# A four-layer graph network: where the own-node terms of two SAGE layers are made, and which engine adds two bias rows

## The chip, the cores and the metric

The kernel runs on one core of one Trainium2 chip. The metric is the device time of the whole program in microseconds, the median of three runs. Three executions took 5216.58, 5223.72 and 5224.33 us.

TensorE multiplies matrices out of SBUF into PSUM, which has eight banks of 512 fp32 columns by 128 partitions. VectorE, ScalarE and GpSimd do the rest; GpSimd issues the indirect DMAs that gather rows. All data here are fp32.

## The reference, cut to what matters

There are 3125 nodes with 128 features and 50000 edges sorted by destination. Four networks follow each other, each with a residual and a layer norm: a message MLP, two graph attention layers, three SAGE layers, and a softmax aggregation with a small MLP. The third and the fourth matter here:

```python
def sage_conv(h, Ws, Wn, b):
    agg = segment_sum(h[edge_src], edge_dst, num_segments=n)
    return h @ Ws + (agg * inv_deg) @ Wn + b
h = relu(sage_conv(x, Ws0, Wn0, b0))     # 128 -> 256
h = relu(sage_conv(h, Ws1, Wn1, b1))     # 256 -> 256
h = relu(sage_conv(h, Ws2, Wn2, b2))     # 256 -> 128
x = layernorm(x + h)
...
h = relu(agg @ mlp_w.T + mlp_b)          # agg: the softmax-weighted sum over a node's edges
x = layernorm(x + (h * scale + x))
```

The own-node terms are `h @ Ws`; they need no neighbour.

## The kernel before, in words

Nodes lie in 26 tiles of 128; features are kept by rows (`x_sb`, `y_sb`, `h_sb`: node on the partition) or turned (`xT` and the six planes of `big`: feature on the partition). Edges lie in 391 blocks of 128. A merge path of 416 steps, 104 groups of four, pairs each block with the node tiles that its edges end in.

**A SAGE pass** (`sum_pass`). GpSimd gathers the source rows of one block with one indirect DMA (L476) from a table in HBM into a ring of 13 groups of four in `big`. Before it refills a ring place it waits on the semaphore `summed`:

```python
if j >= n:
    pool.wait_ge(freed, at + j - n + lag)
```

With n = 13 and a lag of 8, gather group j needs the group six before it to be summed. ScalarE makes, for each step, a 128x128 matrix that marks which edge ends in which node (L882: squared distances, four a group; L888: one minus that, clipped at zero), in two buffers, so it waits for `summed` of the group two back. TensorE multiplies it with the gathered rows (L785) and lets the sums stay in banks 0 to 6 (`node_sums`) over the whole pass. In sage1 the rows have 256 columns; the second half goes through bank 7 (L790), and VectorE adds it to `y_sb` (L1166). In sage0 and sage2 bank 7 and VectorE have nothing to do.

**Between the passes** TensorE fills one of the banks 0 to 3 in turn (`fill`, a ring of four, `RING`), and the engine that the list `STAGES` names for the stage reads it. `fill` waits until the reader of four fills back is done.

- After sage0: VectorE scales the sums (L1537), TensorE turns them (`aT`, L542), ScalarE copies them into `big[0]` (L871). Then `sh0`: 16 fills of 128x416, each of two matmuls, `Ws0` with `xT` and `Wn0` with the turned sums (L533); ScalarE adds the bias `sb0` and clips (L1029) into `big[4]` and `big[5]`. Then `p1`, the products with `Wn1` (L519), copied by ScalarE (L866) and written to HBM as the table of sage1.
- After sage2: VectorE scales the sums of all packs of four tiles (L1537); then `out2`: per tile two products with `Ws2` (L519) and the bias row as a product of a row of ones with `b_sb` (L522); VectorE adds the scaled sums (`join_sage`, L1564) and the residual (`add_residual`, L1569). The layer norm (`norm`) follows: row sum (L1259), centring (L1265), squares on ScalarE (L948), their sum (L1270), square root on ScalarE (L950), scaling into `x_sb` (L1279). `in_packs` runs these steps over seven packs (six of four tiles, one of two) in a staggered order. `x_sb` is then written as the table of the next pass.
- At the end (`last`), per pack: VectorE bounds and inverts the totals (L1579, L1583), divides (L1587); TensorE turns (L830), ScalarE copies (L1049), TensorE multiplies with `mlpT` (L836) and adds the bias row as a product (L837) for each of four tiles; ScalarE clips into `y_sb` (L1050); VectorE scales (`scale_output`, L1593), adds the residuals (`add_both_residuals`, L1597), and the norm follows; the result is written out.

The order on each engine is the order of the code; semaphores tie the engines together. `weights_loaded` counts three loads at the start (16 each): the weights, the two bias rows `b_sb` (1 KB), and `r_sb`, rows spread over all partitions.

## Time and profile before

| | |
|---|---|
| median of three runs | 5223.72 us |
| the profiled execution | 5251.98 us, span 5250.2 us |
| TensorE matmul busy | 3245.7 us (62%) |
| VectorE busy | 2924.6 us (56%) |
| ScalarE busy | 2771.9 us (53%) |
| GpSimd busy | 2886.8 us (55%) |
| pass of sage0 | from 2458.7 to 3042.6 us |
| pass of sage2 | from 3796.0 to 4374.9 us |
| last stretch | from 5172.0 us |

The profile is of one execution. Times in its rows are microseconds from the span's start. A group's idle time is that of its engine just before it, and the name behind the arrow is what ended it; "remote" is a releaser that the profile does not name, "issue" is time in which the engine waited for nothing that it shows. A matmul of fp32 data appears as two records, so x32 are 16 matmuls. PEclk is the granted clock of TensorE as a share of 2.4 GHz; it is 0.5 or 1.0 at any time, and a window's figure is a mean.

### The profile page before, as it was taken

What the parts mean: (1) busy time and instruction counts of PE and PEld (TensorE: products, weight loads), DVE (VectorE), ACT (ScalarE), POOL (GpSimd) and SP (SyncE); (2) the same over time, 40 slices, a digit from 0 to 9 for tenths busy, and PEclk for the clock granted to TensorE, in tenths of its full rate; (3) what the DMA queues carried; (4) which work ended last, traced back from release to release, by engine and by line L of the source; (5) the groups of instructions that cost most, each with busy time, mean ns of one, the idle gap of its engine ahead of it and who ended that gap; (6) DMA issues with size and microseconds to landing.
All of it is one profiled execution on the core that took longest, in us unless ns stands there. A gap on an engine that the chain in (4) does not pass through costs nothing.

```text
span 5250.2 us, 70737 instructions
## 1 busy us (share of the span) xinstructions
PE 3245.7 (62%) x16464; PEld 2658.9 (51%) x16465; DVE 2924.6 (56%) x6078; ACT 2771.9 (53%) x5854; POOL 2886.8 (55%) x2818
## 2 busy tenths in 40 slices
PE   4666667778885778884233364555723335777776
PEld 3555554667774667673223244444522324655554
DVE  3666674999997999996000001112100003999997
ACT  1656664777774777773333333333323332777773
POOL 3455521666663666663666625666166662666661
PEclk7888888665555665555555577777855555999996
DMA  4344421223332323321111122333111111333331
GB/s 141 110 118 120 121 75 35 76 76 78 78 78 52 76 76 77 76 75 42 43 46 47 45 64 76 91 91 89 30 44 46 47 45 39 97 98 96 96 98 30
DMA packets 326787, 385.94 MB, mean 74 GB/s; under 512 B 68200, under 2 KB 267806, under 8 KB 326270
## 3 DMA queue, kind: packets, MB, share of 16 engines
q0 software_dynamic: 102496, 236.78, 16.2%
q1 hardware_dynamic: 221910, 142.28, 9.8%
q10 hardware_dynamic: 2218, 4.94, 0.3%
q8 instruction: 73, 1.20, 0.1%
q14 instruction: 90, 0.74, 0.0%
HBM read 366.52 MB, written 17.21 MB: 73 GB/s over the span
## 4 chain that ended last, share of the span: by engine, by line
PE 31%; another core or an unknown queue 21%; DVE 17%; issue 15%; ACT 11%; DVEq 3%; DMA 1%; SPq 1%; ACTq 0%; POOL 0%
PE ps L737 6%; ACT onehot L882 5%; DVE big L1166 4%; PE ps L595 4%; PE ps L686 3%; PE ps L724 3%; ACT onehot L888 2%; DVE w_run L1344 2%; DVE y_sb L1166 2%; PE ps L716 2%; PE ps L790 2%; PE ps L785 2%; PE ps L519 2%; DVE big L1369 2%
## 5 line engine op out<-in xcount | busy, mean ns | idle before, releaser
L476 POOL DMA_INDIRECT big<-table_sage,src_block x1173 | 1110.3, 947 | 852.5 <-issue 331.6
L462 POOL DMA_INDIRECT rows<-table_gat,src_idx x832 | 924.4, 1111 | 746.3 <-PE ps L659 278.5
L882 ACT ACTIVATE onehot<-iota,dst_rel 128x128 f32<-128x128 f32 x1664 | 530.6, 390 | 1400.5 <-remote 1031.4
L785 PE MATMUL ps<-big,onehot 128*128 x2496 | 536.1, 385 | 789.9 <-ACT onehot L888 459.9
L785 PEld LDWEIGHTS ps<-big,onehot 128*128 128x128 f32 x2496 | 476.2, 283 | 847.2 <-issue 842.5
L737 PE MATMUL ps<-y_sb,onehot 128*128 128x136 f32 (+2 forms) x2496 | 664.2, 425 | 81.5 <-DVE big L1166 73.5
L1537 DVE TENSOR_TENSOR y_sb<-ps,inv_row 128x512 f32<-128x512 f32 (+1 forms) x14 | 8.0, 645 | 1226.3 <-PE ps L785 1226.3
L462 POOL DMA_INDIRECT rows<-table_pool,src_idx x416 | 480.5, 1155 | 311.6 <-PE ps L663 119.6
L1166 DVE TENSOR_TENSOR big<-big,ps 128x257 f32 (+3 forms) x1664 | 576.2, 346 | 87.1 <-PE ps L737 24.9
L737 PEld LDWEIGHTS ps<-y_sb,onehot 128*128 128x128 f32 x2496 | 516.3, 278 | 143.9 <-DVE big L1166 118.0
L476 POOL DMA_INDIRECT big<-table_mlp,src_block x391 | 370.8, 948 | 344.0 <-DVE ps L1186 186.4
L888 ACT ACTIVATE onehot<-onehot,ones 128x512 f32<-128x512 f32 x728 | 524.8, 721 | 13.5
L882 ACT ACTIVATE onehot<-iota,last_rel 128x128 f32<-128x128 f32 x1248 | 398.9, 390 | 245.8 <-PE ps L737 111.0
L1166 DVE TENSOR_TENSOR y_sb<-y_sb,ps 128x128 f32 x416 | 119.5, 287 | 547.6 <-remote 318.1
L1361 DVE TENSOR_TENSOR_SCAN big<-big,ps 128x512 f32<-128x512 bf16 x312 | 395.1, 1266 | 12.7 <-PE ps L663 8.8
L1338 DVE TENSOR_TENSOR_SCAN s_run<-big,s_run 128x512 f32<-128x512 f32 x312 | 398.6, 1278 | 0.0
L1344 DVE TENSOR_TENSOR_SCAN w_run<-big,w_run,y_sb 128x512 f32<-128x512 f32 x312 | 398.3, 1277 | 0.0
L595 PE MATMUL ps<-w_sb,ea_sb 128*128 128x256 f32 x832 | 258.4, 464 | 213.1 <-issue 99.5
L790 PE MATMUL ps<-big,onehot 128*128 x832 | 175.7, 377 | 279.9 <-DVE y_sb L1166 272.8
L989 ACT ACTIVATE big<-big 128x1024 f32<-128x1024 f32 x312 | 330.0, 1058 | 9.8
L686 PE MATMUL ps<-ident,big 128*128 128x128 f32 x832 | 218.3, 413 | 178.3 <-ACT big L968 168.8
L595 PEld LDWEIGHTS ps<-w_sb,ea_sb 128*128 128x128 f32 x832 | 181.3, 229 | 281.5 <-issue 133.0
(231 smaller groups left out, 5925.4 us busy)
## 6 DMA issues: line engine op xcount, KB each, us to landing
ea_sb<-in_ea_blocks SPq DMA_DIRECT2D x832, 64.0 KB
big<-neg_rows SPq DMA_DIRECT2D x312, 128.0 KB
ea_sb<-rel_rows SPq DMA_DIRECT2D x208, 128.0 KB
big<-table_sage,src_block POOLq DMA_INDIRECT x1173
rows<-table_gat,src_idx POOLq DMA_INDIRECT x832
rows<-table_pool,src_idx POOLq DMA_INDIRECT x416
big<-table_mlp,src_block POOLq DMA_INDIRECT x391
w_sb<-in_wpack ACTq DMA_DIRECT2D x1, 2374.0 KB
```

Of the source, the lines that this page charges most:

```text
L462: pool.indirect_dma_start(to[g % 2][:, j, 0:ROW[k]], None, table[k], bass.IndirectOffsetOnAxis(src_idx[:, step:step + 1], 0)).then_inc(loa ...
L476: pool.indirect_dma_start(ring[:, (block + RING_FIRST[k]) % (n * G), :], None, table[k], bass.IndirectOffsetOnAxis(src_block[:, block:bloc ...
L595: mm = pe.matmul(pre(g % 2)[:, j, :], ea_sb[:, g % 2, j, :], weight("W1a", 1), start=True, stop=True)
L686: mm = pe.transpose(ps[:, b, j * P:(j + 1) * P], logit[:, b, j * P:(j + 1) * P], ident[:, :])
L737: mm = pe.matmul(ps[:, 6 + j // 2, (j % 2) * 256:(j % 2) * 256 + width], onehot[:, b, j, :], turned[:, b, j, 0:width], start=True, stop=True)
L785: mm = pe.matmul(to, onehot[:, b, j, :], row(j, 0), start=False, stop=False, skip_group_check=True)
L882: ins = act.activation(onehot[:, b, j, :], iota[:, 0:P], ACT.Square, bias=values[:, bass.ds(x * G + j, 1)], scale=-1.0)
L888: act.activation(onehot[:, b], onehot[:, b], ACT.Relu, bias=ones[:, 0:1], scale=-1.0)\
L1166: dve.tensor_tensor(to, to, bank_of(j), ALU.add).then_inc(accumulated, 1)
L1338: dve.tensor_tensor_scan(s_run[:, b, :], gaps[:, b, 0, :], gaps[:, b, 1, :], s_run[:, 1 - b, G * P - 1:G * P], ALU.mult, ALU.add)
L1344: dve.tensor_tensor_scan(w_run[:, b, :], gaps[:, b, 0, :], hp[:, b, :], w_run[:, 1 - b, G * P - 1:G * P], ALU.mult, ALU.add).then_inc(run_ ...
L1361: dve.tensor_tensor_scan(max_run[:, b, 1:G * P + 1], neg_b[:, b, :], spread_value(b), max_run[:, b, 0:1], ALU.add, ALU.max).then_inc(max_r ...
```

## The change

1. **sage0.** After every sixth group of the pass (g = 5, 11, ..., 95) TensorE makes one of the 16 products of `Ws0` with `xT` (128x416) in bank 7. VectorE adds the bias `sb0` and writes it to `big[4]` or `big[5]`. `sh0` keeps one matmul a fill; VectorE adds the bank to what lies in `big`, and ScalarE clips in place (new semaphore `hidden_ready`, for which `p1` waits). The bias and the sum move from ScalarE to VectorE.
2. **sage2.** After every twelfth group (g = 11, ..., 83) TensorE makes the own terms of one pack (two matmuls a tile) in bank 7; VectorE adds the bias row `sb2` into `y_sb`. The stage `out2` is gone. `join_sage` becomes one instruction a tile: sums from PSUM times the inverse degree plus `y_sb`. The separate scaling after sage2 is gone.
3. **last.** The bias product is gone; VectorE adds the row (`add_mlp_bias`), and the clipping moves from ScalarE into `scale_output`.
4. `b_sb` and its load are gone; `sb2` and `mlp_b` join the spread rows (`r_sb` grows from 768 to 1024 columns).

```diff
-          ("gT", 7, "act"), ("h2", 9, "act"), ("x2T", 7, "act"), ("aT", 7, "act"), ("sh0", 16, "act"), ("p1", 13, "act"),
-          ("sh1", 16, "act"), ("p2", 7, "act"), ("out2", 7, "dve"), ("last", 14, "act")]
-FILLS = [(name, u, who) for name, n, who in STAGES for u in range(n)]
+          ("gT", 7, "act"), ("h2", 9, "act"), ("x2T", 7, "act"), ("aT", 7, "act"), ("sh0", 16, "dve"), ("p1", 13, "act"),
+          ("sh1", 16, "act"), ("p2", 7, "act"), ("last", 14, "act dve")]
+FILLS = [(name, u, who.split()[u % len(who.split())]) for name, n, who in STAGES for u in range(n)]
...
@@ TensorE
                     mm.then_inc(summed, 1)
+                    if k == "sage0" and g % 6 == 5 and g // 6 < 2 * NCOL:
+                        column_self_term(g // 6)
+                    if k == "sage2" and g % 12 == 11 and g // 12 < NPACK:
+                        row_self_term(g // 12)
+
+            def column_self_term(u):
+                if u:
+                    pe.wait_ge(self_read, u)
+                c, m = divmod(u, 2)
+                pe.matmul(ps[:, 7, 0:COLS], weight("Ws0", 0, m * P, P), xT[:, c * COLS:(c + 1) * COLS],
+                          start=True, stop=True).then_inc(self_done, 1)
+
+            def row_self_term(u):
+                pe.wait_ge(self_read, 2 * NCOL + u)
+                for i, t in enumerate(packs(4)[u]):
+                    to = ps[:, 7, i * D:(i + 1) * D]
+                    pe.matmul(to, big[:, 0, pick(t)], weight("Ws2", 0), start=True, stop=False)
+                    mm = pe.matmul(to, big[:, 1, pick(t)], weight("Ws2", 1), start=False, stop=True)
+                mm.then_inc(self_done, 1)
...
-            column_products("sh0", lambda m: [(weight("Ws0", 0, m * P, P), xT),
-                                              (weight("Wn0", 0, m * P, P), sum_T[:, 0, :])])
-            pe.wait_ge(read_by["act"], fills_read(FIRST_FILL["p1"], "act"))
+            column_products("sh0", lambda m: [(weight("Wn0", 0, m * P, P), sum_T[:, 0, :])])
+            pe.wait_ge(hidden_ready, 2 * NCOL)
...
             sum_pass("sage2")
             pe.wait_ge(sums_read, 3 * NPACK)
-            row_products("out2", 4, D, [(big[:, 0, :], weight("Ws2", 0)), (big[:, 1, :], weight("Ws2", 1))],
-                         bias_row("sb2"))
-            pe.wait_ge(read_by["dve"], fills_read(FIRST_FILL["last"], "dve"))
...
-                    to = bank[:, i * D:(i + 1) * D]
-                    pe.matmul(to, xT[:, pick(t)], weight("mlpT", 0), start=True, stop=False)
-                    mm = pe.matmul(to, ones[0:1, :], bias_row("mlp_b"), start=False, stop=True)
+                    mm = pe.matmul(bank[:, i * D:(i + 1) * D], xT[:, pick(t)], weight("mlpT", 0), start=True, stop=True)
@@ ScalarE
-            relu_columns("sh0", "sb0", 4)
+            for c in range(NCOL):
+                for m in range(2):
+                    at = big[:, 4 + m, c * COLS:(c + 1) * COLS]
+                    act.wait_ge(read_by["dve"], fills_read(FIRST_FILL["sh0"] + 2 * c + m + 1, "dve"))
+                    act.activation(at, at, ACT.Relu).then_inc(hidden_ready, 1)
...
-                act.activation(y_flat[:, at], filled("last", 2 * u + 1)[:, 0:len(tiles) * D], ACT.Relu)\
-                   .then_inc(read_by["act"], 1)
@@ VectorE
+            for u in range(2 * NCOL):
+                c, m = divmod(u, 2)
+                dve.wait_ge(self_done, u + 1)
+                dve.tensor_scalar(big[:, 4 + m, c * COLS:(c + 1) * COLS], ps[:, 7, 0:COLS],
+                                  weight("sb0", 0)[:, m:m + 1], None, ALU.add).then_inc(self_read, 1)
             sum_pass("sage0")
...
+            dve.wait_ge(self_read, 2 * NCOL)
+            for u in range(2 * NCOL):
+                c, m = divmod(u, 2)
+                at = big[:, 4 + m, c * COLS:(c + 1) * COLS]
+                dve.tensor_tensor(at, filled("sh0", u)[:, 0:COLS], at, ALU.add).then_inc(read_by["dve"], 1)
...
+            for u, tiles in enumerate(packs(4)):
+                dve.wait_ge(self_done, 2 * NCOL + u + 1)
+                row = spread("sb2").unsqueeze(1).to_broadcast([P, len(tiles), D])
+                bank = ps[:, 7, 0:len(tiles) * D].rearrange("p (t f) -> p t f", f=D)
+                dve.tensor_tensor(y_sb[:, of_pack(u), :], bank, row, ALU.add).then_inc(self_read, 1)
+            dve.wait_ge(self_read, 2 * NCOL + NPACK)
             sum_pass("sage2")
-            for u in range(NPACK):
-                scaled_sums(u, y_sb).then_inc(sums_scaled, 1)
-            dve.wait_ge(sums_scaled, NPACK)
-            dve.sem_inc(sums_read, NPACK)
 
             def join_sage(u):
-                dve.tensor_tensor(y_sb[:, of_pack(u), :], bank_rows("out2", u), y_sb[:, of_pack(u), :], ALU.add)\
-                   .then_inc(read_by["dve"], 1)
+                for t in packs(4)[u]:
+                    ins = dve.scalar_tensor_tensor(y_sb[:, t, :], node_sums[:, t, :], inv_row[:, t:t + 1], y_sb[:, t, :],
+                                                   ALU.mult, ALU.add)
+                ins.then_inc(sums_read, 1)
...
+            def add_mlp_bias(u):
+                bank = filled("last", 2 * u + 1)[:, 0:len(packs(4)[u]) * D].rearrange("p (t f) -> p t f", f=D)
+                row = spread("mlp_b").unsqueeze(1).to_broadcast([P, len(packs(4)[u]), D])
+                dve.tensor_tensor(y_sb[:, of_pack(u), :], bank, row, ALU.add).then_inc(read_by["dve"], 1)
+
             def scale_output(u):
-                dve.wait_ge(read_by["act"], fills_read(FIRST_FILL["last"] + 2 * u + 2, "act"))
+                dve.wait_ge(read_by["dve"], fills_read(FIRST_FILL["last"] + 2 * u + 2, "dve"))
                 row = spread("scale").unsqueeze(1).to_broadcast([P, len(packs(4)[u]), D])
-                dve.tensor_tensor(y_sb[:, of_pack(u), :], y_sb[:, of_pack(u), :], row, ALU.mult).then_inc(y_half, 1)
+                dve.scalar_tensor_tensor(y_sb[:, of_pack(u), :], y_sb[:, of_pack(u), :], 0.0, row, ALU.max, ALU.mult)\
+                   .then_inc(y_half, 1)
...
-            norm(4, bound_totals, invert_totals, divide, pause, scale_output, add_both_residuals)
+            norm(4, bound_totals, invert_totals, divide, pause, add_mlp_bias, scale_output, add_both_residuals)
```

## Rows read from the trace of the kernel before

**Rows 1.** Windows by stage: two tails and the last stretch; busy us (instructions) by engine.
```profile
core 0: us, PE busy (x) PEld busy (x) DVE busy (x) ACT busy (x) POOL busy (x), PEclk, DMA share, GB/s
3042.50:3076.30 33.80, 28.42 (x90) 17.48 (x90) 6.84 (x8) 13.57 (x23) 0.00 (x0) 0.90 0.00 0
4374.90:4434.60 59.70, 48.77 (x156) 37.04 (x156) 24.82 (x44) 4.42 (x8) 0.00 (x0) 0.52 0.00 0
5172.00:5240.60 68.60, 44.84 (x130) 30.53 (x130) 47.78 (x58) 13.43 (x23) 0.00 (x0) 0.50 0.00 0
```

**Rows 2.** Windows of 300 us inside the passes of sage0 and sage1; same columns.
```profile
2600.00:2900.00 300.00, 98.84 (x416) 86.05 (x416) 0.00 (x0) 101.24 (x256) 198.09 (x211) 0.56 0.16 46
3300.00:3600.00 300.00, 164.87 (x832) 150.06 (x832) 58.58 (x204) 102.03 (x256) 194.99 (x207) 0.74 0.31 91
```

**Rows 3.** Waits of GpSimd in 500 us of sage0, sage1, sage2: total, times, longest.
```profile
POOL big L476 <- remote: 61.6, 24, 3.2
...
POOL big L476 <- remote: 77.7, 39, 2.0
...
POOL big L476 <- remote: 63.2, 17, 4.0
```

**Rows 4.** Timeline inside sage2's pass: start, duration, engine, line, idle before.
```profile
3917.36 2.04 PE L785 MATMUL ps<-big,onehot 128*128 x8 [9.29 <-issue]
...
3924.83 1.28 ACT L882 ACTIVATE onehot<-iota,dst_rel 128x128 f32<-128x128 f32 x4 [7.87 <-remote]
3925.07 0.94 POOL L476 DMA_INDIRECT big<-table_sage,src_block  x1 [3.91 <-remote]
```

**Rows 5.** Timeline behind sage0's pass.
```profile
3052.99 0.97 PE L533 MATMUL ps<-xT,w_sb 128*128 128x416 f32 x2 [0.53 <-ACT big L871]
...
3075.65 0.61 ACT L1029 ACTIVATE big<-ps,w_sb 128x416 f32<-128x416 f32 x1 [0.79 <-PE ps L533]
...
3076.31 3.95 PE L519 MATMUL ps<-w_sb,big 128*128 128x256 f32 x17 [0.70 <-ACT big L1029]
```

**Rows 6.** Timeline behind sage2's pass.
```profile
4374.92 4.01 DVE L1537 TENSOR_TENSOR y_sb<-ps,inv_row 128x512 f32<-128x512 f32 x7 [642.36 <-PE ps L785]
...
4379.04 1.22 PE L519 MATMUL ps<-w_sb,big 128*128 128x128 f32 x4 [4.24 <-DVEq L1561]
...
4380.19 0.79 PE L522 MATMUL ps<-b_sb,ones 1*128 1x128 f32 x2
...
4431.84 0.68 DVE L1270 TENSOR_REDUCE stat<-big 128x4 f32<-128x512 f32 x1
...
4432.43 0.42 DVE L1265 SCALAR_TENSOR_TENSOR y_sb<-stat,y_sb 128x256 f32<-128x256 f32 x1
...
4432.76 1.01 DVE L1270 TENSOR_REDUCE stat<-big 128x4 f32<-128x512 f32 x2
...
4434.63 4.04 DVE L1279 SCALAR_TENSOR_TENSOR x_sb<-y_sb,stat 128x512 f32<-128x512 f32 x7
```

**Rows 7.** Timeline of the last stretch.
```profile
5184.48 1.11 PE L830 MATMUL ps<-ident,y_sb 128*128 128x128 f32 x4
...
5186.43 3.34 DVE L1583 RECIPROCAL big<-big 128x512 f32<-128x512 f32 x1
...
5192.13 1.11 PE L830 MATMUL ps<-ident,y_sb 128*128 128x128 f32 x4
...
5238.20 1.01 DVE L1270 TENSOR_REDUCE stat<-big 128x4 f32<-128x512 f32 x2
...
5240.65 4.04 DVE L1279 SCALAR_TENSOR_TENSOR x_sb<-y_sb,stat 128x512 f32<-128x512 f32 x7
```

**Rows 8.** Groups by form over the span: busy us, mean ns, idle before.
```profile
L1166 DVE TENSOR_TENSOR y_sb<-y_sb,ps 128x128 f32 x416 | 119.5, 287 | 547.6 <-remote 318.1 <-PE ps L790 169.0 <-issue 14.7
```

**Rows 9.** Gather instructions in 300 us of sage1: ns min/median/max.
```profile
L476 POOL DMA_INDIRECT big<-table_sage,src_block x207: 943/949/958, 3299.5 to 3599.8; - x104
```

**Rows 10.** Timeline at the kernel's start.
```profile
22.16 12.87 PE L519 MATMUL ps<-w_sb,xT 128*128 128x256 f32 x52 [3.54 <-DVE big L1090]
```

More of the change, by code:

```diff
@@ L42 @@
            "mlpT": (1, 128), "b2a": (1, 2), "sb0": (1, 2), "sb1": (1, 2)}
-BIAS_ROWS = {"sb2": 128, "mlp_b": 128}
-SPREAD_ROWS = {"b1a": 256, "b2b": 128, "gb1": 128, "gb2": 128, "scale": 128}
+SPREAD_ROWS = {"sb2": 128, "mlp_b": 128, "b1a": 256, "b2b": 128, "gb1": 128, "gb2": 128, "scale": 128}
 def offsets(sizes):
@@ L57 @@
 W_AT, W_COLS = offsets({k: c * n for k, (c, n) in WEIGHTS.items()})
-B_AT, B_COLS = offsets(BIAS_ROWS)
 R_AT, R_COLS = offsets(SPREAD_ROWS)
@@ L106, with program @@
 RING_COUNT = ring_counts()
-def program(nc, edges_i, src_blocks, ea_blocks, x_rows, xT_in, wpack, bpack, rpack, out):
+def program(nc, edges_i, src_blocks, ea_blocks, x_rows, xT_in, wpack, rpack, out):
     with ExitStack() as ctx:
@@ L128, in program @@
         w_sb = sb("w_sb", [P, W_COLS])
-        b_sb = sb("b_sb", [1, B_COLS])
         r_sb = sb("r_sb", [P, R_COLS])
@@ L283, in program @@
         out_written = sem("out_written")
+        self_done, self_read, hidden_ready = sem("self_done"), sem("self_read"), sem("hidden_ready")
         gathered = [sem("gathered0"), sem("gathered1")]
@@ L543, in turn_rows @@
                     mm.then_inc(fill_done, 1)
-            pe.wait_ge(weights_loaded, 48)
+            pe.wait_ge(weights_loaded, 32)
             pe.wait_ge(x_loaded, 16)
@@ L818, in _ @@
             row_products("p2", 4, D, [(big[:, 0, :], weight("Wn2", 0)), (big[:, 1, :], weight("Wn2", 1))], None)
-            pe.wait_ge(read_by["act"], fills_read(FIRST_FILL["out2"], "act"))
+            pe.wait_ge(read_by["act"], fills_read(FIRST_FILL["last"], "act"))
             sum_pass("sage2")
             pe.wait_ge(sums_read, 3 * NPACK)
-            row_products("out2", 4, D, [(big[:, 0, :], weight("Ws2", 0)), (big[:, 1, :], weight("Ws2", 1))],
-                         bias_row("sb2"))
-            pe.wait_ge(read_by["dve"], fills_read(FIRST_FILL["last"], "dve"))
             softmax_pass("pool")
@@ L1106, in filled @@
                 return ps[:, n % RING, :]
-            dve.wait_ge(weights_loaded, 48)
+            dve.wait_ge(weights_loaded, 32)
             for u, tiles in enumerate(packs(2)):
@@ L1555, in _ @@
             dve.sem_inc(acc_zeroed, 1)
-            dve.wait_ge(read_by["act"], fills_read(FIRST_FILL["out2"], "act"))
+            dve.wait_ge(read_by["act"], fills_read(FIRST_FILL["last"], "act"))
+            for u, tiles in enumerate(packs(4)):
[4 more added lines that the diff above has]
+            dve.wait_ge(self_read, 2 * NCOL + NPACK)
             sum_pass("sage2")
-            for u in range(NPACK):
-                scaled_sums(u, y_sb).then_inc(sums_scaled, 1)
-            dve.wait_ge(sums_scaled, NPACK)
-            dve.sem_inc(sums_read, NPACK)
             def join_sage(u):
-                dve.tensor_tensor(y_sb[:, of_pack(u), :], bank_rows("out2", u), y_sb[:, of_pack(u), :], ALU.add)\
-                   .then_inc(read_by["dve"], 1)
+                for t in packs(4)[u]:
+                    ins = dve.scalar_tensor_tensor(y_sb[:, t, :], node_sums[:, t, :], inv_row[:, t:t + 1], y_sb[:, t, :],
+                                                   ALU.mult, ALU.add)
+                ins.then_inc(sums_read, 1)
             def add_residual(u):
-                dve.wait_ge(read_by["dve"], fills_read(FIRST_FILL["out2"] + u + 1, "dve"))
+                dve.wait_ge(sums_read, 2 * NPACK + u + 1)
                 dve.scalar_tensor_tensor(y_sb[:, of_pack(u), :], y_sb[:, of_pack(u), :], 0.0, x_sb[:, of_pack(u), :],
@@ L1645, in lay_out @@
         cols.append(weights[name].reshape(c, P, m).transpose(1, 0, 2).reshape(P, c * m))
-    bias = {"sb2": a["L2_gnn_b2"],
-            "mlp_b": a["L3_gnn_mlp_b"]}
-    spread = {"b1a": a["L0_gnn_b1a"], "b2b": a["L0_gnn_b2b"], "gb1": head_last(a["L1_gnn_b1"], 0), "gb2": a["L1_gnn_b2"], "scale": a["L3_gnn_scale"]}
+    spread = {"sb2": a["L2_gnn_b2"], "mlp_b": a["L3_gnn_mlp_b"],
+              "b1a": a["L0_gnn_b1a"], "b2b": a["L0_gnn_b2b"], "gb1": head_last(a["L1_gnn_b1"], 0), "gb2": a["L1_gnn_b2"], "scale": a["L3_gnn_scale"]}
     return {
@@ L1651, in lay_out @@
         "wpack": np.ascontiguousarray(np.concatenate(cols, axis=1)),
-        "bpack": np.concatenate([bias[k].reshape(-1) for k in BIAS_ROWS]).reshape(1, -1),
         "rpack": np.concatenate([spread[k].reshape(-1) for k in SPREAD_ROWS]).reshape(1, -1),
```

4 lines of the change are left out of this document (removed).

## The prediction, made before the result was known

> **What bounds the kernel now.** I read the page first: no engine is busy through the span, so the time lies in stages with different limits. I cut the part of the span that the edit touches into its stages by windows [rows 1], then took windows inside the passes, the list of waits, and the timeline at each edge.
>
> The gather passes of sage0 and sage2 come first. GpSimd issues a gather every 300 / 211 = 1.42 us in sage0, and TensorE works a third of the time there at a mean granted clock of 0.56 [rows 2]. GpSimd's own step is 1.25 us (0.95 busy, 0.30 issue); the rest is pauses: 61.6 us in 24 waits in 500 us of sage0, 63.2 us in 17 waits in sage2, one every five groups or so [rows 3]. The releaser is not named, but line 472 waits on `summed` alone, which TensorE raises. In the excerpt of sage2 the same release starts ScalarE's next markers at 3924.83 and GpSimd's gather at 3925.07, 5 us after TensorE had ended the group that began at 3917.36 [rows 4]. So the passes are bound by GpSimd plus a late release of `summed`, and not by how much TensorE computes.
>
> Behind each pass there is a stretch without a gather. After sage0, TensorE is the bound: 32 matmuls of 416 columns from 3052.99 to 3075.6, 0.70 us each, with ScalarE close behind and `p1` waiting for the last of them [rows 5]. After sage2, VectorE scales the sums for 4.0 us, and then TensorE works at granted clock 0.5 (1.2 GHz): 48.77 us busy for 26 tiles, 1.87 us each [rows 1], of which products 1.15 (4379.04 to 4380.19) and the one-row bias 0.72, with the layer norm trailing it [rows 6]. VectorE is busy for only 24.8 of 59.7 us there [rows 1]. In the last stretch each pack costs TensorE 7.65 us (5184.48 to 5192.13), of which four bias matmuls are 4 x 0.72 = 2.9 us [rows 7]; VectorE is busy for 47.8 of 68.6 us [rows 1].
>
> **Layer 0's tail.** Half of the 32 matmuls leave it. TensorE starts at 3052.99 as before; 32 steps end at 3075.6, when ScalarE's last Relu starts [rows 5], so 16 of 0.70 us and the same 0.2 us of start and drain end at 3064.4. Then VectorE's add of 128x416 (0.57 us, between 0.42 for 256 columns and 0.68 for 512 [rows 6]) and ScalarE's Relu in place (0.61 us, as L1029 [rows 5]) follow in series, with about 0.1 us of waits: `p1` starts at 3065.8 instead of 3076.31. Both need less than 0.70 us a fill, so TensorE stays the bound, also through the ring of four banks. Gain 10.5 us. The step of 0.70 us is that of the full clock, to which the marking-bound end of the pass had brought TensorE (0.90 over this stretch [rows 1]); the pass's end is not altered. At half clock 16 steps of 1.40 us would give the whole gain back. The clearing of `y_sb` (L1156) now waits behind the 16 adds on VectorE; its first reader comes only after `p1`, some 35 us later, so it stays hidden.
>
> **Layer 2's tail.** `out2` goes entirely: 26 x 1.87 = 48.6 us of TensorE. What is left is VectorE's own chain. From neighbours in one queue: 0.60 us a step at 128x512 and 0.34 at 128x256 (durations 0.68 and 0.42, while the starts 4431.84, 4432.43 and 4432.76 lie 0.59 and 0.33 apart: an overlap of 0.08 [rows 6]). The new join is 26 instructions of 128x128; at 0.287 us each [rows 8], less the same overlap, 0.21 us. A full pack then costs 4 x 0.21 + 4 x 0.60 = 3.2 us (join, residual, row sum, centre, sum of squares), six of them 19.4, the half pack 1.8: 21.2 us. From the last reduce (4432.76 + 1.01) to x_sb at 4434.63 it is 0.9 us as before [rows 6]; I allow 0.3 us for starts. The start stays 4374.92, so x_sb comes at 4397.3: gain 37.3 us. Bounds: no overlap between the narrow joins (+2.1), or a wait of 0.07 more each (+4).
>
> A rule of the Trainium skill speaks against the narrow joins. Rows first: 512 columns cost 0.68 us and 128 cost 0.287 us [rows 6, 8], so four narrow ones carry some 0.45 us more work than a wide one. The Trainium skill, VectorE: DVE Perf Modes, section on the TRN2 errata, says that a fixed latency is paid per instruction and gives 120 cycles plus the elements for a PSUM source, so 0.26 us for each of these. By that, an estimate, the 26 would take 6.7 us and the gain would be 36.0 us instead of 37.3.
>
> **The last stretch.** TensorE's pack falls from 7.65 to 4.8 us. VectorE then sets the pace: per pack the bound of the totals (0.28, L1579), the reciprocal (3.27, from 3.34 less the overlap) and seven steps of 0.60, one more than before: 7.75 us; six are 46.5, the half pack, at about half the reciprocal and 0.34 a step, 4.2: 50.7 us. Between divide(u) and the new add_mlp_bias(u) VectorE does two reciprocals and more, 7.7 us; TensorE and ScalarE need transposes 1.1, copy 0.75, four products 2.9, that is 4.9 us, so nothing waits. The scaling loads ScalarE's square root table late, as now; I keep the present 1.5 us from the last reduce (5238.20 + 1.01) to x_sb, and allow 0.3 us for starts. The stretch begins at 5172.0 [rows 1]: 5172.0 + 50.7 + 1.8 = 5224.5, against 5240.65 [rows 7]: gain 16.1 us. If VectorE waited once in each of seven packs for 0.6 us, 4 us less.
>
> **What the passes pay.** Sage0 gets 16 matmuls of 416 columns, 1.40 us each at half clock (0.70 [rows 5] doubled), 22.3 us, and 16 evacuations of about 0.6 us. Sage2 gets 26 pairs of 1.15 us, 29.9 us, and seven evacuations. VectorE idles there now [rows 2]. The insert stands behind `summed` in TensorE's queue; behind it are the next group's matmuls. Sage1 is the nearest row for TensorE time added to such a pass: per gather 164.87 / 207 = 0.796 us of TensorE against 98.84 / 211 = 0.468, and 1.449 us against 1.422 [rows 2]. So 0.33 us more TensorE cost 0.027 us, or 8%. That makes 1.9 + 2.5 = 4.4 us. Ends: nothing; or all 52.2 us, if a group that starts late moves the pauses by as much. I take the row, since sage1 also has twice the bytes and VectorE's adds.
>
> The other rule weighed: in sage1, with VectorE busy for 58.6 of 300 us, a gather instruction still takes 943 to 958 ns [rows 2, 9]. The Trainium skill, SBUF — State Buffer, section on the two separate sides, says that GpSimd cannot write descriptors while VectorE holds their shared port in a fast two-port mode. By that rule a clash costs at most one VectorE instruction of 0.6 us, 23 of them 14 us, against nothing by the row; the added instructions all read PSUM, and no run here shows the rule.
>
> **Start.** The 1 KB load is gone and the spread rows grow by 128 KB. TensorE's first products at 22.16 are released by VectorE's L1090, not by the weights [rows 10]; I take zero, with 0.5 us either way.
>
> **Sum.** 10.5 + 37.3 + 16.1 = 63.9; less 4.4 it is 59.5 us. The profiled execution took 5251.98 us (span 5250.2 and 1.8 around it), so 5192.5. It lies 28 us above the median of the timed runs, 5223.72; the difference is carried over: 5164 us.
>
> **Rivals.**
> - *The passes pay TensorE's time in full.* For: ScalarE's markers, and through them TensorE, already stand on the chain in the passes. Against: the 8% of sage1. Between half and all of 52 us: 5186 to 5212.
> - *The passes gain.* `summed` is released late where TensorE has run dry [rows 3, 4]; more work in its queue might bring the release forward, or a shift break the pattern. If every second insert spares a pause of 3.7 us (63.2 / 17), 12 x 3.7 = 44 us: 5120; a few spared, 5145.
> - *Slower: each insert costs one more pause.* GpSimd waits for a group six back; the insert makes that group late by 1.4 or 4.6 us, just when its credit has run out. 23 x 3.7 = 85 us against 63.9: 5245. It decides from 2.8 us per insert (63.9 / 23), where all is lost. Against it: a pause comes once in some 20 gathers, and sage1, with a longer group every time, shows 39 waits with 77.7 us in 500 us against 24 with 61.6 [rows 3]: 16 us more for some 85 longer groups, 0.2 us each.
> - *Layer 0's tail runs at half clock.* Costs 11 us: 5175.
>
> **Chances and range.** Forecast 0.66, its own range 5156 to 5174 from the bounds above; passes pay in full 0.14; passes gain 0.12; half clock 0.04; slower by the pauses 0.04. The range for 8 in 10 reaches into the two neighbours: 5138 to 5192. A measurement of this kernel tells 0.2%, 10 us, from no change. Faster by more: 0.93; within: 0.03 (most of a full payment together with a lost term); slower: 0.04.
>
> **What would show it.** The first `p1` product some 23 us after the pass's last sum instead of 34; x_sb of layer 2 about 22 us behind the pass's last sum; the last stretch about 52 us long with VectorE without gaps and TensorE at under 5 us a pack; the two passes at 1.42 to 1.44 us a gather. A rate of 1.50 us or more, or GpSimd pauses above 80 us in 500, would mean that the inserts are paid and the prediction is wrong in the passes.

## The result, and the profile after

The changed kernel took 5153.81 us (median of four, 5148.52 to 5153.93), the kernel before 5224.02 us beside it. The ratio is 0.9871, with a 95% interval from 0.986 to 0.9883: a gain of 61 to 73 us, 70.2 by the medians. The forecast was 5164 us and a gain of 59.5, in a range of 5138 to 5192.

The profiled execution of the changed kernel took 5153.76 us with a span of 5151.8, 98.4 less than the span of before. The three stretches that the edit shortens and the two passes show in the windows of the changed kernel: start and end, length, then busy us and instructions of TensorE, its weight loads, VectorE, ScalarE and GpSimd, granted clock, DMA share, GB/s.

```profile
core 0: us, PE busy (x) PEld busy (x) DVE busy (x) ACT busy (x) POOL busy (x), PEclk, DMA share, GB/s
3019.70:3042.90 23.20, 17.03 (x59) 11.34 (x59) 13.47 (x23) 12.67 (x23) 0.00 (x0) 0.85 0.00 0
4327.20:4350.70 23.50, 0.00 (x0) 0.00 (x0) 23.07 (x57) 4.42 (x8) 0.00 (x0) 0.55 0.00 0
5090.10:5142.30 52.20, 20.66 (x78) 16.20 (x78) 51.20 (x66) 9.45 (x16) 0.00 (x0) 0.51 0.00 0
2600.00:2900.00 300.00, 103.61 (x442) 87.84 (x442) 5.85 (x9) 104.05 (x265) 198.91 (x212) 0.58 0.18 46
3300.00:3600.00 300.00, 173.11 (x846) 157.51 (x846) 59.67 (x208) 103.93 (x260) 197.20 (x209) 0.68 0.32 92
```

The first three rows answer to [rows 1]. The stretch behind layer 2 fell from 59.7 to 23.5 us and VectorE fills 23.07 of them; the last stretch fell from 68.6 to 52.2 us and VectorE fills 51.20. TensorE, 44.84 us busy in the last stretch before, is down to 20.66. The fourth row answers to the first of [rows 2]: with the insertions in it, GpSimd still issues 212 gathers in 300 us against 211. So the passes paid nothing that this row can show.

Behind sage0's pass, in the timeline of the changed kernel (start, duration, engine, line, idle before):

```profile
3019.76 4.01 DVE L1544 TENSOR_TENSOR y_sb<-ps,inv_row 128x512 f32<-128x512 f32 x7 [16.80 <-PE ps L778]
...
3030.19 2.01 PE L526 MATMUL ps<-big,w_sb 128*128 128x416 f32 x5 [0.74 <-ACT big L876]
...
3042.30 0.55 ACT L1048 ACTIVATE big<-big 128x416 f32<-128x416 f32 x1 [0.15 <-DVE big L1562]
3042.90 0.92 PE L512 MATMUL ps<-w_sb,big 128*128 128x256 f32 x3 [1.26 <-ACT big L1048]
```

From the first `sh0` product to `p1` it is 12.71 us, against 23.32 in [rows 5]; from the scaling to `p1` 23.1 us. Behind sage2's pass:

```profile
4327.24 1.13 DVE L1584 SCALAR_TENSOR_TENSOR y_sb<-ps,inv_row,y_sb 128x128 f32<-128x128 f32 x4 [73.03 <-PE ps L778]
4328.40 0.69 DVE L1590 SCALAR_TENSOR_TENSOR y_sb<-y_sb,x_sb 128x512 f32<-128x512 f32 x1
4329.01 1.12 DVE L1584 SCALAR_TENSOR_TENSOR y_sb<-ps,inv_row,y_sb 128x128 f32<-128x128 f32 x4
4330.05 0.68 DVE L1266 TENSOR_REDUCE stat<-y_sb 128x4 f32<-128x512 f32 x1
...
4350.69 1.90 DVE L1286 SCALAR_TENSOR_TENSOR x_sb<-y_sb,stat 128x512 f32<-128x512 f32 x3
```

x_sb comes 23.45 us behind the pass, against 59.71 in [rows 6]. Four narrow joins step in 1.04 us (4329.01 to 4330.05), 0.26 us each.

In the last stretch TensorE and ScalarE wait for VectorE, which itself waits only once, at the end, 0.88 us for the square root:

```profile
5102.46 0.68 DVE L1614 TENSOR_TENSOR y_sb<-ps,r_sb 128x512 f32<-128x512 f32 x1
5103.06 0.68 DVE L1608 TENSOR_TENSOR y_sb<-big 128x512 f32<-128x512 f32 x1
5103.66 3.35 DVE L1604 RECIPROCAL big<-big 128x512 f32<-128x512 f32 x1
5103.89 1.08 PE L838 MATMUL ps<-ident,y_sb 128*128 128x128 f32 x4 [0.82 <-DVE y_sb L1608]
5105.01 0.60 ACT L1058 ACTIVATE xT<-ps 128x512 f32<-128x512 f32 x1 [4.13 <-PE ps L838]
5105.75 2.05 PE L843 MATMUL ps<-w_sb,xT 128*128 128x128 f32 x8 [0.78 <-ACT xT L1058]
```

From the transposes to the end of the products it is 3.9 us a pack (5103.89 to 5107.80). In [rows 7] it was 7.65 us from one pack's transposes to the next one's, and TensorE worked through nearly all of them.

GpSimd's waits in the same 500 us of sage0 and of sage2 as in [rows 3], changed kernel (total, times, longest):

```profile
POOL big L469 <- remote: 64.3, 25, 3.8
...
POOL big L469 <- remote: 64.3, 20, 4.0
```

61.6 and 63.2 us before, 64.3 and 64.3 after: the pauses are as they were. The two profiles alone leave one thing open. The three stretches gave 10.6 + 36.3 + 16.5 = 63.4 us, but the span fell by 98.4. The rest came from stages that the edit touches little or not at all: 16.5 us before the first gather of sage0, 6.3 and 7.0 in the two passes, 7.2 from sage1's first gather to sage2's; the softmax aggregation between layer 2's tail and the last stretch was 2.1 us longer.

### The profile page after: what moved, and what is told of

It reads as the page before. It is cut to its first block, busy times and chain, and to the rows that moved or that the text cites. A ratio compares the mean times of both kernels' runs of the same rounds, so it can differ in the third digit from the quotient of the medians.

```text
span 5151.8 us, 70579 instructions
## 1 busy us (share of the span) xinstructions
PE 3180.4 (62%) x16360; PEld 2605.6 (51%) x16361; DVE 2945.7 (57%) x6136; ACT 2766.6 (54%) x5847; POOL 2908.0 (56%) x2818
## 4 chain that ended last, share of the span: by engine, by line
PE 28%; another core or an unknown queue 21%; DVE 20%; issue 16%; ACT 9%; DVEq 3%; DMA 1%; POOL 0%; ACTq 0%; SPq 0%; POOLq 0%
PE ps L730 6%; DVE big L1173 5%; ACT onehot L887 4%; PE ps L588 3%; DVE w_run L1351 3%; PE ps L778 3%; PE ps L679 3%; PE ps L717 2%; DVE y_sb L1173 2%; PE ps L709 2%; ACT onehot L893 2%; DVE big L1376 2%; PE ps L783 2%; DVE h_sb L1201 1%
## 5 line engine op out<-in xcount | busy, mean ns | idle before, releaser
L455 POOL DMA_INDIRECT rows<-table_gat,src_idx x832 | 950.5, 1142 | 710.0 <-DMA table_gat<-h_sb 249.2
L1551 DVE TENSOR_SCALAR big<-ps,w_sb 128x416 f32<-128x416 f32 x16 | 10.4, 650 | 550.5 <-remote 372.6
```

The costliest lines, as they stand in the source:

```text
L455: pool.indirect_dma_start(to[g % 2][:, j, 0:ROW[k]], None, table[k], bass.IndirectOffsetOnAxis(src_idx[:, step:step + 1], 0)).then_inc(loa ...
```

## The experiments

Stage lengths below are differences of starts in the profiled execution of each kernel: a pass from its first gather to VectorE's first instruction behind it, layer 0's tail from there to `p1`, layer 2's tail from there to x_sb, the last stretch from the first bounding of the totals to x_sb. By this measure the pass of sage2 in the kernel before starts at 3788.7 us, its first gather, and not at 3796.0 as in the table of the profile before. The first four kernels ran on a chip on which the kernel before took 4735.8 us; the other eight on chips where it took 5217.0 to 5220.7. A kernel is compared only with the kernel before on its own chip.

**One part at a time.** First, layer 0 alone, on the kernel before:

```diff
+                    if k == "sage0" and g % 6 == 5 and g // 6 < 2 * NCOL:
+                        column_self_term(g // 6)
...
+            column_products("sh0", lambda m: [(weight("Wn0", 0, m * P, P), sum_T[:, 0, :])])
+            pe.wait_ge(hidden_ready, 2 * NCOL)
```

> The kernel before with only the first part of the change: the own-node terms of layer 0 in its pass, the sum and the bias on VectorE. Before took 5224.0 us. Theory A, the prediction's terms as measured: the tail gives 10.6 us, the 16 inserts cost 0 to 1.9 us: 5213.4 to 5215.3 us. Theory B, the inserts spare GpSimd some of its pauses, which would explain why the whole change gave 70.2 us instead of 59.5: its share would be about 6 us more (the pass was 6.3 us shorter in the profile), 5207 us. Theory C, the inserts are paid in full and something else gains: 22.3 us of inserts against 10.6, 5236 us.

Measured: 4724.91 against 4735.82 us, minus 10.9; ratio 0.9977 (0.9968 to 0.9986). Its tail is 23.2 us.

Second, layer 2 alone (`row_self_term`, the bias row and the narrow join in; `out2` and the separate scaling out):

```diff
+                    if k == "sage2" and g % 12 == 11 and g // 12 < NPACK:
+                        row_self_term(g // 12)
...
-            row_products("out2", 4, D, [(big[:, 0, :], weight("Ws2", 0)), (big[:, 1, :], weight("Ws2", 1))],
-                         bias_row("sb2"))
```

> The kernel before with only the second part: the own-node terms and the bias row of layer 2 in its pass, the stage behind the pass gone, the join as one instruction a tile. Theory A: the tail gives 36.3 us, the seven inserts cost 0 to 2.5: 5187.7 to 5190.2 us. Theory B, the inserts spare pauses: the pass was 7.1 us shorter in the profile, so 5180.6 us. Theory C, paid in full: 29.9 against 36.3, 5217.6 us.

Measured: 4699.23 us, minus 36.6; ratio 0.9922 (0.9909 to 0.9936). Its tail is 23.44 us, and 59.7 in the two kernels of this chip that keep `out2`.

Third, the last bias row alone, with the clipping moved from ScalarE into VectorE's scaling as in the change:

```diff
-                    mm = pe.matmul(to, ones[0:1, :], bias_row("mlp_b"), start=False, stop=True)
+                    mm = pe.matmul(bank[:, i * D:(i + 1) * D], xT[:, pick(t)], weight("mlpT", 0), start=True, stop=True)
...
+            norm(4, bound_totals, invert_totals, divide, pause, add_mlp_bias, scale_output, add_both_residuals)
```

> The kernel before with only the third part: the bias row of the last MLP added by VectorE, the clipping in the scaling. No pass is touched. Theories A and B: 16.5 us of gain by the last stretch of the two profiles, 5207.5 us. If it comes out at 5202 us or less, part of the unexplained 10.7 us lies here and not in the passes.

Measured: 4718.35 us, minus 17.5; ratio 0.9965 (0.9953 to 0.9977). Its last stretch is 52.14 us against 68.6.

What follows: each part gives what its own stretch gives, and 10.9 + 36.6 + 17.5 = 65.0 us is their sum. Theory B (pauses spared) wanted some 13 us more in layers 0 and 2 together, theory C (insertions paid in full) a loss of 12 us in the first; neither came. This chip could not test B well, though: in the passes GpSimd has no pause to spare. Windows of 300 us in sage0, sage1 and sage2 of the kernel with layer 0 alone:

```profile
2300.00:2600.00 300.00, 134.22 (x502) 107.88 (x502) 6.50 (x10) 119.85 (x300) 226.84 (x240) 0.52 0.21 53
2850.00:3150.00 300.00, 173.87 (x959) 160.19 (x957) 68.79 (x240) 119.93 (x300) 227.05 (x240) 0.77 0.37 105
3450.00:3750.00 300.00, 122.97 (x483) 107.04 (x483) 0.00 (x0) 119.84 (x300) 226.87 (x241) 0.50 0.21 53
```

All three go at 300 / 240 = 1.25 us a gather, GpSimd's own step, sage1 with its longer groups too. In [rows 2] it was 1.42 us in sage0 and 1.45 in sage1.

**The products twice.** Each own-node product of the changed kernel is made twice in its place:

```diff
+                for _ in range(2):
+                    mm = pe.matmul(ps[:, 7, 0:COLS], weight("Ws0", 0, m * P, P), xT[:, c * COLS:(c + 1) * COLS],
+                                   start=True, stop=True)
...
-                for i, t in enumerate(packs(4)[u]):
+                for i, t in list(enumerate(packs(4)[u])) * 2:
```

> The changed kernel with every own-node product in the two passes made twice (same bank, same result; 52.2 us more of TensorE at half clock, in the same 23 places). After took 5153.8 us. Theory A, 8 in 100 of TensorE's time is paid: plus 4.4, 5158 us. Theory C, paid in full: plus 52, 5206 us. Theory B, more work in TensorE's queue brings the release of the other engines forward and spares pauses: minus up to 10, 5144 us.

Measured: 4672.37 us, minus 63.4; ratio 0.9866 (0.9851 to 0.9881). The comparison on the same chip is with the sum of the parts, 65.0. Its passes take 502.7 and 504.5 us; with single insertions 504.2 (layer 0 alone) and 504.6 (layer 2 alone), without any 503.1 and 504.4 to 504.6 (the kernels that leave them out). The insertions cost nothing here, single or double, although they ran at half clock: the median record of the 16 products of sage0 lasts 901 ns with single and with double insertions.

**Before and after once more.** Both word for word, on a chip where the kernel before takes 5218.0 us.

> The kernel before once more, word for word, for a second profile of it. The first four experiments ran on a chip where before took 4735.8 us instead of 5224.0 and where GpSimd had no pauses without a named releaser in the passes. Theory P, the pauses belong to the chip and not to the kernel: on a chip where the time is near 4736 us they are absent from the passes of sage0 and sage2, which take about 503 and 504 us; near 5224 us they are there. Theory Q, they belong to this kernel's order of events and the edits removed them: they are there on any chip, and the passes are longer than 575 us.

Measured: 5221.42 against 5218.00 us of the runs beside it; ratio 1.0004 (0.9994 to 1.0014). The span of its profile is 5211.1, not 5250.2. In 500 us of sage0 GpSimd's waits are

```profile
POOL big L476 <- issue: 96.9, 318, 0.3
POOL big L476 <- remote: 63.2, 26, 3.7
```

so the pauses are there. On the chip of 4735.8 us the kernel with the last bias row alone, whose passes are those of the kernel before, has no such wait in its passes. Together that is theory P: the pauses come with the chip. The passes of this profile take 578.4 and 577.7 us.

> The changed kernel once more. The parts alone gave 10.9, 36.6 and 17.5 us, 65.0 together. Theory A, the parts are independent and the passes pay nothing: before minus 65.0 us, and within 2 us of the kernel with its terms made twice (minus 63.4). If the 70.2 us of the first comparison were due to pauses spared on that chip (theory B), a chip with pauses shows about 70 and one without shows 63 to 65.

Measured: 5156.55 us, minus 61.5; ratio 0.9881 (0.9864 to 0.9898). Theory B wanted about 70 on a chip with pauses. Side by side, in us:

| profiled execution | up to sage0's first gather | pass of sage0 | tail of layer 0 | sage1's first to sage2's first gather | pass of sage2 | tail of layer 2 | last stretch |
|---|---|---|---|---|---|---|---|
| before | 2458.8 | 583.7 | 33.8 | 684.9 | 586.2 | 59.7 | 68.6 |
| before, again | 2442.3 | 578.4 | 32.9 | 677.7 | 577.7 | 59.7 | 68.6 |
| after | 2442.3 | 577.5 | 23.1 | 677.7 | 579.2 | 23.4 | 52.1 |
| after, again | 2443.7 | 578.5 | 23.2 | 678.5 | 579.0 | 23.4 | 52.1 |

The odd one out is the first profile of before: longer by 5.3 to 16.5 us in each of the four columns with gathers in them, edited or not. Against its repeat the passes are the same within 1.5 us, and what is left is the three stretches: 62.5 us by the table, where the spans differ by 59.3.

**Without the insertions.** The changed kernel without its 23 insertions. VectorE's reads of bank 7 stay, but nothing paces them now: their waits for TensorE go with the insertions (also cut here), so they run at the start of a pass, and one product of zeros fills the bank once ahead of them. The own-node terms are missing from the result.

```diff
-                    if k == "sage0" and g % 6 == 5 and g // 6 < 2 * NCOL:
-                        column_self_term(g // 6)
-                    if k == "sage2" and g % 12 == 11 and g // 12 < NPACK:
-                        row_self_term(g // 12)
```

> The changed kernel without the 23 insertions of TensorE in the two passes: the own-node terms of layers 0 and 2 are left out of the result, and VectorE reads bank 7 as it is. Theory A, the inserts cost nothing measurable: within 2 us of the changed kernel. With the 8 in 100 of the prediction: 4.4 us faster. Paid in full: 52 us faster. If the inserts spare pauses: slower by up to 10 us on a chip with pauses, and the same on one without.

Measured: 5152.98 us, 3.6 below the changed kernel beside it, with ratios to before of 0.9870 (0.9854 to 0.9887) and 0.9881 (0.9864 to 0.9898), so not to be told apart; 4.4 us would not be either. Its passes take 578.2 and 581.4 us, no shorter than with the insertions. Fully paid insertions are excluded.

**Eight times.** As the kernel with the products twice, with 8 for 2.

> The changed kernel with every own-node product of the two passes made eight times (same bank, same result): an insertion of TensorE lasts 11.2 us in layer 0 and some 37 us in layer 2, each at half clock (half of that at the full clock). Theory M, a margin: GpSimd waits only for the group six back, 25 to 30 us of gathering, and TensorE needs 2 to 3 of each group's 5 us, so it catches up; an insertion is free up to some 20 us and paid beyond it: layer 0 still pays nothing, layer 2 pays 7 x 17 = 120 us at half clock, nothing to 30 at the full clock. Rival 8, eight in a hundred of the added time (365 us beyond the changed kernel) is paid in both passes: 29 us, 13 of it in layer 0. Rival full: 365 us.

Measured: 5222.61 us, 66 above the changed kernel (5156.55), 64 by the two ratios; ratio to before 1.0003 (0.9995 to 1.0012). Sage0's pass takes 582.7 us, where kernels with single insertions show 577.4 to 582.4, and sage2's 640.9 against 579: 62 us. One insertion of sage2, TensorE and GpSimd in the timeline of this kernel:

```profile
3996.21 0.39 PE L803 MATMUL ps<-w_sb,big 128*128 128x128 f32 x2
...
4028.37 2.28 PE L778 MATMUL ps<-big,onehot 128*128 x16
```

```profile
4012.15 0.95 POOL L469 DMA_INDIRECT big<-table_sage,src_block  x1 [0.31 <-issue]
4029.70 0.94 POOL L469 DMA_INDIRECT big<-table_sage,src_block  x1 [16.60 <-PE ps L778]
```

TensorE is away for 32.2 us (3996.21 to 4028.37). GpSimd gathers on for 16.9 of them (to 4013.1), then stands for 16.6 with TensorE as the named releaser. The seven insertions last 33.2, 28.4, 32.2, 26.7, 29.0, 30.0 and 23.5 us, 29 in the mean, and cost 62 / 7 = 8.9: about 20 us of each are free. That is theory M, whose 120 us assumed half clock throughout. What fills the insertions is another matter. The one above in three windows:

```profile
3996.21:3999.45 3.24, 3.24 (x31) 3.24 (x30) 0.00 (x0) 0.39 (x1) 2.51 (x3) 1.00 0.23 61
3999.45:4016.54 17.09, 5.52 (x17) 3.84 (x16) 0.00 (x0) 2.00 (x5) 10.41 (x11) 0.65 0.17 46
4016.54:4028.37 11.83, 11.83 (x85) 11.82 (x85) 0.00 (x0) 0.00 (x0) 0.00 (x0) 0.78 0.01 1
```

For 17.09 us in its middle TensorE is busy for only 5.5, and the profile names nothing that it waits for. All seven insertions have such stretches: TensorE is busy for 137 of their 202 us. So the 29 us are the time for which TensorE is away from the pass, and not the price of the products. Three of the insertions also show how late `summed` acts. In the second one TensorE ends its group and starts the insertion, in which it raises nothing, and both engines that wait for `summed` are released in the middle of it (TensorE, ScalarE, GpSimd):

```profile
3917.14 2.04 PE L778 MATMUL ps<-big,onehot 128*128 x8 [6.72 <-issue]
...
3928.82 1.28 ACT L889 ACTIVATE onehot<-iota,dst_rel 128x128 f32<-128x128 f32 x4 [12.04 <-remote]
...
3929.06 0.94 POOL L469 DMA_INDIRECT big<-table_sage,src_block  x1 [3.75 <-remote]
```

The group ended at 3919.18, the release came 9.6 us later, at the time when TensorE's records turn dense again. The prediction's late release is thus seen directly. What causes it, and whether the thin stretches have the same cause, stays open.

Eight in a hundred of what was really added (16 insertions of 5.75 us instead of 0.70 in sage0, 203 us in all instead of some 18 in sage2) would be 6 us in sage0, which the spread does not exclude, and 15 in sage2, a quarter of what was paid. In sage2's pass GpSimd's waits are

```profile
POOL big L469 <- PE ps L778: 94.3, 10, 16.8
POOL big L469 <- remote: 44.4, 13, 3.8
```

against 14.6 and 64.3 us in the changed kernel: 80 us more of named waits, 20 us less of pauses. Longer insertions do take the place of pauses, but never for a net gain.

**A wide join.** The join of layer 2 as a scaling and an addition of 512 columns a pack:

```diff
-                for t in packs(4)[u]:
-                    ins = dve.scalar_tensor_tensor(y_sb[:, t, :], node_sums[:, t, :], inv_row[:, t:t + 1], y_sb[:, t, :],
-                                                   ALU.mult, ALU.add)
-                ins.then_inc(sums_read, 1)
+                scaled_sums(u, spare_rows).then_inc(sums_scaled, 1)
...
+                dve.tensor_tensor(y_sb[:, of_pack(u), :], spare_rows[:, of_pack(u), :], y_sb[:, of_pack(u), :], ALU.add)\
+                   .then_inc(sums_read, 1)
```

> The changed kernel with the join of layer 2 as two wide instructions a pack (scaling into a spare plane, then the addition of the own-node terms) instead of one narrow instruction a tile. By the trace of the changed kernel four narrow ones step in 1.03 us and two wide ones should in 1.20: plus 0.17 us a pack, 1.1 us over 6.5 packs, and one more step of delay at the end is covered by the order: x_sb 24.6 us behind the pass instead of 23.45. If an instruction's fixed part weighed no more than the prediction's 0.21 us a tile, it would be plus 0.36 a pack, 25.8 us.

Measured in the timeline: x_sb 24.60 us behind the pass, as expected from 0.26 us a narrow join. The whole, 5153.17 us and ratio 0.9869 (0.9855 to 0.9884), can't show 1 us.

**More off VectorE.** Both shortened stretches are VectorE's own chain now, so work was taken off it. The sums of squares first, in all four layer norms of the program:

```diff
-                    at = pack_columns(u)
-                    act.activation(spare[:, at], y_flat[:, at], ACT.Square).then_inc(squared, 1)
+                    for t in packs(4)[u]:
+                        at = slice(t * D, (t + 1) * D)
+                        ins = act.activation(spare[:, at], y_flat[:, at], ACT.Square, accum_out=stat[:, 2, t:t + 1])
+                    ins.then_inc(squared, 1)
...
-                in_packs(*makers, sum_rows_of, center, pause, sum_squares)
+                in_packs(*makers, sum_rows_of, center)
```

> The changed kernel with the sum of squares of all four layer norms taken by ScalarE, one Square a tile with its accumulated output, in place of seven wide Squares on ScalarE and seven reductions on VectorE. Theory V, VectorE's own chain sets the stretch behind layer 2 and the last stretch: each gets shorter by the 6.5 steps of 0.60 us that leave VectorE, 3.9 us, 23.45 to 19.6 and 52.1 to 48.2 us; with the two earlier norms up to 15.6 us in all. Rival W, ScalarE's 26 narrow Squares (some 0.35 us each, 1.4 a pack, plus the reading of the accumulator) become the bound or trail behind: the last pack ends 1 to 2 us later, gain 5 us or less.

Measured: 5145.49 us, 11.1 below the changed kernel beside it; ratio 0.9859 (0.9843 to 0.9876). Behind layer 2 20.8 us instead of 23.4, in the last stretch 50.0 instead of 52.1. Of the 3.9 us that theory V gave each, 1.2 and 1.7 went to the trail of ScalarE's squares behind the last pack (rival W). These two stretches hold 4.8 us of the 11. The two earlier layer norms hold another 4.2: from the first row sum to x_sb they take 14.5 and 21.8 us in this trace and 16.6 and 24.0 in the changed kernel's. The last 2 us are within the spread.

Then the bias row laid into PSUM by ScalarE, with TensorE's products added to it, and the root's table loaded ahead of the squares:

```diff
+                act.activation(bank, r_sb[:, R_AT["mlp_b"]:R_AT["mlp_b"] + D].unsqueeze(1).to_broadcast([P, len(tiles), D]),
+                               ACT.Copy).then_inc(bias_laid, 1)
...
-                    mm = pe.matmul(bank[:, i * D:(i + 1) * D], xT[:, pick(t)], weight("mlpT", 0), start=True, stop=True)
+                    mm = pe.matmul(bank[:, i * D:(i + 1) * D], xT[:, pick(t)], weight("mlpT", 0), start=False, stop=True,
+                                   skip_group_check=True)
...
+                link(act.activation(root_sink[:, :], ones[:, 0:1], ACT.Sqrt))
```

> The changed kernel with three things moved off VectorE or off the end of the norm: the sums of squares on ScalarE as in the run before (minus 2.65 us behind layer 2, minus 2.2 in the last stretch); the bias row of the last MLP laid into PSUM by ScalarE, with TensorE's products added to it, so that VectorE loses one of its steps of 0.60 us a pack; and one small square root ahead of the squares, so that its table is loaded while ScalarE waits and not behind the last square (1.28 us). Theory V, VectorE's own chain sets both stretches: the last one 49.96 - 3.9 - about 1 = 45 us, the one behind layer 2 20.8 - about 1 = 19.7 us; the whole kernel 17 to 21 us below the changed one, of which 11 were seen with the squares alone. Rival X, the laying of the row waits for VectorE's reading of the bank two packs back and makes TensorE late: the last stretch stays at 48 us or more.

Measured: 5138.74 us; ratio 0.9845 (0.9833 to 0.9858). The last stretch is 47.0 us, between V (45) and X (48); the one behind layer 2 stays at 20.8, since there the table had been loaded already. ScalarE's timeline shows what holds the last stretch:

```profile
5106.05 0.38 ACT L1074 ACTIVATE xT<-ps 128x256 f32<-128x256 f32 x1 [0.69 <-PE ps L844]
5106.45 1.28 ACT L958 ACT_TABLE_LOAD   x1
5107.74 0.20 ACT L958 ACTIVATE root_sink<-ones 128x1 f32<-128x1 f32 x1
5107.98 0.31 ACT L963 ACTIVATE big<-y_sb 128x128 f32<-128x128 f32 x1
```

All 26 squares stand behind the last copy and the table; from 5107.98 to 5115.7 they run without a gap, 0.29 us each (not the 0.39 of the next expectation), and VectorE waits 3.1 us for the last. So their order was changed:

```diff
+            load_root()
             for u, tiles in enumerate(packs(4)):
...
+                if u >= 5:
+                    squares(4, u - 5)
+            norm(4, NPACK - 5)
```

> The run before last (sums of squares and bias row on ScalarE) with another order on ScalarE: in the last stretch its squares came only behind all seven copies, so that 26 of them, 0.39 us each, trailed VectorE by 3.1 us, and the root's table was loaded between copies and squares. Here the root's table is loaded ahead of the copies, and the squares of the first two packs stand behind the sixth and the seventh copy. Theory V, VectorE's chain then sets the stretch: 47.0 minus 1.3 for the table and some 1 us of the trail, 44.5 to 45 us. Rival Y, ScalarE's rate of 1.57 us a pack against VectorE's last steps still holds the end: 46 us or more. The rest of the kernel as before; the whole some 2 us below the last one's ratio of 0.9845, 0.984.

Measured in the trace: the last stretch is 45.1 us, as theory V has it. The whole is 5138.01 us with a ratio of 0.9846 (0.9832 to 0.9859), where the run before had 0.9845: 2 us are below what the timing tells. By the ratios both versions lie 13 to 19 us below the changed kernel.

## Why the prediction was right, point by point

- *Layer 0's tail*, 10.5 us: 10.6 by the first pair of profiles, 9.7 by the second, 10.9 timed alone. TensorE's 16 steps at 0.70 us set it, and VectorE's addition and ScalarE's Relu kept up with them. The half-clock rival is out: the granted clock was 0.85 in that stretch.
- *Layer 2's tail*, 37.3 us: 36.3, and 36.6 timed alone. x_sb came 23.45 us behind the pass where 22.4 was forecast. The term that was mis-sized is the narrow join: 0.26 us a tile, not the 0.21 that came from taking the same overlap off 0.287 [rows 8]; 26 x 0.05 = 1.3 us. The overlap was right and the instruction was not: the join, which reads a third operand, lasts 0.34 us, and the addition of [rows 8] 0.287. The Trainium skill, VectorE: DVE Perf Modes, section on the TRN2 errata, gives 0.26 us for such an instruction, from which the prediction had estimated a gain of 36.0: the trace agrees for these, with a step of 0.26 us and a gain of 36.3, and the wide join, at 24.60 us, bears the step out. For 512 columns out of PSUM the trace does not agree: the scalings behind sage0's pass (L1544, six wide and one half in 4.01 us) step in 0.60 us, where the same formula would give 0.66, an estimate.
- *The last stretch*, 16.1 us: 16.5, and 17.5 timed alone. VectorE is the bound, and TensorE's pack takes 3.9 us instead of the 4.9 allowed: its four products take 2.05 us and not 2.9.
- *What the passes pay*, 4.4 us: nothing that can be measured, by the stage table, by the kernel without insertions and by the products twice. This is the one step whose reasoning failed. It read the difference of 1.449 and 1.422 us a gather between sage1 and sage0 as the price of TensorE's time. On the chip without pauses the passes go at 1.25 us alike, though TensorE is busy for 0.72 us a gather in sage1 and for 0.51 in sage2 (173.87 / 240 and 122.97 / 241). So the difference lay in the pauses, of which sage1 had 77.7 us in 500 and sage0 61.6 [rows 3], and short insertions pay no share of TensorE's time. They lie in the slack of the six groups by which GpSimd may run ahead; the insertions of 29 us put that slack at some 20 us, with only the excess paid. That is one size of insertion, and none between 5.75 and 23 us was tried. Nor did sage0's insertions take 22.3 us on the slower chips: most ran at the full clock, 0.70 us each. The line view of the changed kernel (ns min, median and max of one record) has a median of 515 where half clock shows 901:

```profile
L794 PE MATMUL ps<-xT,w_sb x32: 512/515/901, 2515.0 to 3001.8; 128*128 128x416 f32 x32
```

- *The rule on the shared port*, weighed and given no share of the sum: 212 gathers in 300 us with nine of VectorE's evacuations beside them against 211 without bears out nothing, as taken. Whether a single one clashed no run shows.
- *The base.* Carrying the 28 us by which the first profile lay above the median was right: the repeat is 39 us shorter, and its three stretches are as long as before to within 0.9 us, so the excess lay outside what the edit shortens.
- *The size.* 59.5 us forecast, 70.2 and then 61.5 timed; the stretches sum to 62.5 to 63.4. The forecast was low by the 4.4 us of the passes and by the small errors above (+0.1, -1.0, +0.4). The remainder of the first figure is not explained by the kernel: its interval reaches from 61 us, and the second one from 53 to 71.
- *The rivals.* "Passes pay in full" fails on the repeats and on the products twice; "passes gain" on the same pauses before and after; "one more pause each" as well, and by the slack of some 20 us an insertion would cost the named 2.8 us only when it lasts about 23, an estimate from the eightfold insertions.

## What to carry to other kernels

Work that is ready early can be put behind a queue that runs ahead of its consumer, at no price that could be measured here, as long as one insertion is shorter than the lead that is left when it begins. The credit bounds it from above (six groups of 5.7 us, 34 us); what was left was less, GpSimd gathering on for 16.9 us in the insertion shown and some 20 us being free in the mean. Look for such a lead before taking a price from the ratio of two stages. After such a move, look at once for the engine that is now without gaps: here it was VectorE in both stretches, and two steps of 0.60 us a pack taken off it, with the root's table loaded earlier, shortened the last stretch from 52.1 to 45.1 us once ScalarE's squares no longer trailed behind. A second profile of the kernel before is worth having: one execution was 39 us longer than its repeat, spread over stages that could have been credited to the edit.

## What the runs showed of the hardware that was not expected

The same program took 4735.8 us on one chip and 5217.0 to 5220.7 us on others, 10% more. On the slower ones GpSimd stands for 60 to 65 us in 500 of sage0 or sage2 without a named releaser, in pauses of up to 4.4 us, and gathers every 1.42 us; on the faster one there is no such wait, and it gathers every 1.25 us. The gather instruction takes 944 to 947 ns in the mean on both. What holds back the release on the slower chips no run told apart. The profiles of the slower chips also hold fewer semaphore events (32,548 to 33,716 against 77,856 to 77,892), so a missing name alone says little; the slower step and the releases inside the long insertions are what shows the pauses.

In the long insertions of sage2 TensorE did not issue its products without gaps, and its granted clock moved with what it did. In the one at 3996.21 a pair of records took 0.39 us at first, at the full clock; after the 17 us with 5.5 us of work a pair took 0.64 us, the half clock; and from 4021.89 on, with the products running without a gap since 4016.54, it took 0.39 us again.
